# A one-core decoder layer: the convolution kernel's prologue in overlapping quarters, x loaded ahead of a zero fill, and the experts in groups of two and two batches instead of three and one

## The chip, the cores and the metric

One core of one Trainium2 chip runs the whole program in one launch. The metric is the device time of that launch in microseconds, the median of several runs. The kernel before takes 579.54 us (three runs, 575.65 to 581.82).

## The reference, cut to what matters

Four batches of 512 tokens of width 128 go through one decoder layer:

```python
y  = attention(x)            # 16 heads of 8, 4 KV heads, RMS-normed and rotated q/k, tanh soft cap 50, causal
x1 = layernorm(x + y)
# cross attention to 32 context rows -> FiLM scale and shift, on a state-space (S4D) long convolution
K  = 2 * Re(sum_n dC[d,n] * exp(dtA[d,n] * l))          # l = 0..511, the convolution kernel, from weights only
t  = causal_conv(modulate(layernorm(x1)), K) ...        # in the kernel: discrete Fourier transform, lags, back
h  = layernorm(t); ff = W2 gelu(W1 h); x2 = layernorm(...)
# mixture of experts: two shared experts on all tokens, 2 of 8 routed experts for each token
out = layernorm(x2 + shared(x2) + w_a * expert_a(x2) + w_b * expert_b(x2))
```

All of it is computed in both kernels. Nothing of the arithmetic's result is changed.

## The kernel before, in words

**Orders written out by hand.** Each of the four compute engines plays a list of named steps (`PE_ORDER`, `ACT_ORDER`, `DVE_ORDER`, `POOL_ORDER`, lines 75 to 183). A step is a small function with its own semaphore waits. An engine works strictly in the order of its list, so a step that waits holds all that stand behind it. `sc:b.p.n` is a fill of scores of batch b, head pair p; `tanh`, `exp` and `mask` are the softmax of that pair on ScalarE and GpSimd; `val:q` multiplies the probabilities of two pairs by the values; `xT`, `qkv`, `rms`, `rope`, `parts`, `copies`, `qT` prepare a batch; `rows`, `y`, `yT`, `proj`, `x1` finish its attention; `xs`, `attnT`, `film`, `mod`, `dft`, `lags`, `conv`, `shape` are cross attention, FiLM and the convolution; `h`, `hT`, `up`, `down`, `ffT`, `ffn`, `x2` the feed-forward; `gates`, `route`, `rank`, `place`, `scatter` the routing; `su`, `sd` the eight steps of the two shared experts; `bt`, `bu`, `bd` (transpose, up, down) with `bx`, `bg`, `by`, `store` are one block of 128 rows of a routed expert; `fetch`, `fin`, `settle`, `fo` gather and finish a batch. `val:15` is the last of the attention.

**The prologue of the convolution kernel.** K is built in four quarters q of 32 channels. GpSimd makes the angles (`angles`, L1019) and the exponents (`exps`, L1037), VectorE reduces the angles (`args`, L1303), ScalarE takes three sines and two exponentials (`powers`, L882), VectorE mixes (`powers`, L1318), GpSimd multiplies (`products`, L1029), TensorE multiplies 32 small matrices (`taps`, L632) and VectorE copies the result into `kij` (L1296). Angles and exponents share the tiles `pr` and `ue`, so that the exponents of a quarter wait for its `args`, and the angles of the next quarter for the `products`. After the fourth quarter SyncE writes `kij` to memory (256 KB) and reads it back in another layout. `tap` (L1340) builds the transform's tables and adds one row, `kernel:0/1` transform K, `spectra` and `spectra2` make the three spectra that `lags` needs. No batch can go past `dft` and `lags` without them.

**The loads.** SyncE issues all loads from one queue in the order of the code (L474 is the helper). x of batches 2 and 3 and the feed-forward weights `wt` stand behind a zero fill of 8.9 MB of `expert_rows`, the memory that the routed tokens are scattered to.

**The experts.** `GROUP = [0, 0, 0, 1]` (L53) runs the routed experts twice: for batches 0 to 2, and for batch 3. A group of n batches has `2 * n * SEQ / P + NE - 1` blocks (L57), the most that the routing can need: 31 and 15, 46 in all. SyncE loads a group's blocks (weights of 578 KB and rows of 64 KB for each, from six slots) once the group's block table is written and its last scatter has landed:

```python
            for g in range(GROUPS):
                sp.wait_ge(table_ready, g + 1)
                sp.wait_ge(scattered[g], 16 * 2 * NT * SIZE[g])
                for q in range(NB[g]):
                    load_block(BLOCK0[g] + q)
```

The block buffers share memory with tiles of the attention, so no block is loaded before `val:15` (L562). The gathers of a group's batches (`fetch`, L1115) wait for the stores of all its blocks.

## Time and profile before

| | |
|---|---|
| median of three runs | 579.54 us (575.65 to 581.82) |
| the profiled execution | 581.24 us, of which 579.5 us are the span that the profile shows |
| TensorE matmuls busy | 429.5 us (74%) |
| VectorE busy | 374.5 us (65%) |
| ScalarE busy | 328.0 us (57%) |
| GpSimd busy | 263.2 us (45%) |
| mean granted TensorE clock | 0.873 of full speed |
| memory traffic | 58.58 MB, mean 101 GB/s |

The profiled execution is one run, 1.7 us above the median of the three. Busy shares are averages over stages that differ: attention of batches 0 to 2 lies between 45 and 244 us of the span, that of batch 3 between 244 and 338 us, the routed experts from 422 us on.

### The profile page before, as it was taken

Reading aid. Unit: us, or ns where it says so; the run is one execution under the profiler, and the core shown is the slowest. Engines: PE = TensorE matmul, PEld = TensorE weight load, DVE = VectorE, ACT = ScalarE, POOL = GpSimd, SP = SyncE. Lnnn points to the kernel's source line nnn. Section 1 sums busy time; section 2 is a strip of 40 time slices with the busy share of each in tenths; the row PEclk is TensorE's granted clock in tenths of the full one; section 3 lists DMA queues with packets and bytes.
Section 4 is the critical chain, followed back from the end, with each engine's and each line's share of the span. In section 5 each row is a group of like instructions: output and inputs, shape, how many; then the busy total and the mean of one; then the engine's idle time right before and its main releaser. Section 6 shows DMA issues by size and latency. Waiting matters only on the chain.

```text
span 579.5 us, 9129 instructions
## 1 busy us (share of the span) xinstructions
PE 429.5 (74%) x2857; PEld 272.5 (47%) x2857; DVE 374.5 (65%) x1107; ACT 328.0 (57%) x563; POOL 263.2 (45%) x305
## 2 busy tenths in 40 slices
PE   3475646763776967789887988988888899888860
PEld 2252223440333624344333446455757887877750
DVE  1993885269872787887899599788711438124554
ACT  1046979895798798637784743614235356444420
POOL 2400876359694372244177645642610123107753
PEclk9977767786878687989877999999979999999985
DMA  3595000000000069400000100100178996888931
GB/s 99 170 421 220 2 1 3 0 1 0 1 2 1 1 156 195 89 2 0 2 1 0 37 2 1 36 2 0 38 235 255 303 307 196 282 284 260 315 88 41
DMA packets 43814, 58.58 MB, mean 101 GB/s; under 512 B 7531, under 2 KB 32870, under 8 KB 43750
## 3 DMA queue, kind: packets, MB, share of 16 engines
q1 hardware_dynamic: 35094, 50.78, 28.7%
q0 software_dynamic: 2048, 4.20, 2.4%
q10 hardware_dynamic: 6624, 3.02, 1.8%
q8 instruction: 24, 0.39, 0.3%
q14 instruction: 24, 0.20, 0.1%
HBM read 42.23 MB, written 20.46 MB: 108 GB/s over the span
## 4 chain that ended last, share of the span: by engine, by line
PE 28%; DVE 21%; SPq 12%; POOL 11%; ACT 10%; DMA 9%; issue 9%; POOLq 0%; DVEq 0%; ACTq 0%
SPq L474 9%; PE bank_o L699 6%; DMA x_blk<-expert_rows 5%; ACT probs L917 3%; PE ring_g L777 3%; PE ring_g L579 3%; DMA x<-in_x 3%; PE ring_g L782 2%; PE ring_s L685 2%; POOL probs L1071 2%; PE ring_g L749 2%; ACT probs L923 2%; PE ring_s L850 2%; SPq L555 2%; SPq L553 2%
## 5 line engine op out<-in xcount | busy, mean ns | idle before, releaser
L917 ACT ACTIVATE probs<-ring_s 128x512 f32<-128x512 f32 (+1 forms) x192 | 87.6, 542 | 38.7 <-PE ring_s L685 36.9
L1071 POOL TENSOR_SCALAR_AFFINE_SELECT probs<-probs 128x256 f32<-128x256 f32 (+1 forms) x96 | 54.6, 601 | 96.5 <-ACT probs L923 96.5
L966 ACT ACTIVATE g_ring<-ring_s,w_blk 128x128 f32<-128x128 f32 x184 | 52.0, 372 | 57.2 <-PE ring_s L850 51.3
L685 PE MATMUL ring_s<-qT,kT 64*128 64x256 bf16 (+3 forms) x256 | 55.3, 350 | 31.5 <-ACT probs L917 29.0
L923 ACT ACTIVATE probs<-probs 128x2560 f32<-128x2560 f32 x32 | 75.1, 2345 | 0.7
L699 PE MATMUL bank_o<-probs,vv 128*32 128x128 f32 (+3 forms) x512 | 55.1, 588 | 22.8 <-POOL probs L1071 22.6
L1017 POOL TENSOR_TENSOR rstd<-var_eps,neg_half 128x4 f32<-128x4 f32 x24 | 25.1, 1047 | 83.8 <-DVE var_eps L1379 75.9
L685 PEld LDWEIGHTS ring_s<-qT,kT 64*128 64x128 bf16 x256 | 16.2, 98 | 74.5 <-ACT probs L917 54.7
L850 PE MATMUL ring_s<-xT_blk,w_blk 128*128 128x128 f32 x368 | 48.3, 277 | 1.7 <-DVE xT_blk L1682 1.7
L858 PE MATMUL ring_g<-w_blk,g_ring 128*128 128x128 f32 x368 | 48.1, 277 | 0.6 <-ACT g_ring L966 0.6
L699 PEld LDWEIGHTS bank_o<-probs,vv 128*32 128x32 f32 x512 | 20.7, 138 | 57.1 <-issue 54.6
L1125 POOL DMA_INDIRECT y_pair<-expert_out,y_rows x32 | 30.9, 967 | 34.6 <-DMA expert_out<-y_blk 25.5
L850 PEld LDWEIGHTS ring_s<-xT_blk,w_blk 128*128 128x128 f32 x368 | 44.5, 192 | 4.1 <-issue 3.8
L1112 POOL DMA_INDIRECT expert_rows<-x,rows_i x32 | 31.6, 986 | 31.9 <-DVE rows_i L1661 23.3
L858 PEld LDWEIGHTS ring_g<-w_blk,g_ring 128*128 128x128 f32 x368 | 44.3, 192 | 1.9 <-issue 1.4
L959 ACT ACTIVATE g_ring<-ring_s,vcols 128x512 f32<-128x512 f32 x32 | 21.5, 690 | 38.2 <-PE ring_s L823 21.8
L1688 DVE TENSOR_TENSOR y_blk<-ring_g,w_blk 128x128 f32<-128x128 f32 x46 | 13.2, 289 | 34.4 <-PE ring_g L858 34.3
L1682 DVE COPY xT_blk<-ring_g 128x128 f32<-128x128 f32 x46 | 13.1, 287 | 33.1 <-PE ring_g L579 33.0
L832 PEld LDWEIGHTS bank_a<-w_sh,g_ring 128*128 128x128 f32 x256 | 30.8, 192 | 4.3 <-issue 4.3
L832 PE MATMUL bank_a<-w_sh,g_ring 128*128 128x128 f32 x256 | 31.7, 275 | 0.0
L823 PE MATMUL ring_s<-x2T,w_sh 128*128 128x512 f32 x64 | 31.3, 599 | 0.0
L579 PE MATMUL ring_g<-ident,x 128*128 128x128 f32 x48 | 8.9, 316 | 22.8 <-DMA x<-in_x 9.6
(342 smaller groups left out, 915.3 us busy)
## 6 DMA issues: line engine op xcount, KB each, us to landing
w_blk<-expert_pack SPq DMA_DIRECT2D x46, 578.0 KB, 5.1
expert_rows<-zero_rows SPq DMA_DIRECT2D x1, 6144.0 KB, 20.7
expert_pack<-in_L_ffn_W SPq DMA_DIRECT2D x16, 256.0 KB
x_blk<-expert_rows SPq DMA_DIRECT2D x46, 64.0 KB, 4.4
expert_out<-y_blk ACTq DMA_DIRECT2D x46, 64.0 KB, 4.7
expert_rows<-zero_rows SPq DMA_DIRECT2D x1, 2048.0 KB, 19.1
x<-in_x SPq DMA_DIRECT2D x4, 256.0 KB, 8.9
w_sh<-in_L_ffn_sW SPq DMA_DIRECT2D x4, 256.0 KB, 4.8
```

The source lines that it names most:

```text
L474: sp.dma_start(dst, src).then_inc(s, 16)
L685: last = mm(bank[:, c:c + w], kT[64 * r:64 * r + 64, p // 2, P * j:P * (j + 1)], qT[64 * r:64 * r + 64, p, P * j:SEQ], start=True, stop=True)
L699: last = mm(bank_o[32 * h:32 * h + 32, P * j:SEQ], vv[:, j, q, :], probs[:, (2 * quad + h // 2) % NPROB, c:c + SEQ - P * j], start=(j == 0 ...
L823: mm(bank[:, :], w_sh[:, e, P * n:P * (n + 1)], x2T[:, b, :], start=True, stop=True).then_inc(s_full, 1)
L832: last = mm(bank_a[:, P * j:P * (j + 1)], g[:, P * j:P * (j + 1)], w_sh[:, e, HID + P * n:HID + P * (n + 1)], start=(c == 0 and j == 0), s ...
L850: last = mm(bank[:, P * n:P * (n + 1)], w_blk[:, k % SLOTS, P * n:P * (n + 1)], xT_blk[:, k % RING, :], start=True, stop=True)
L858: last = mm(bank[:, 0:D], g[:, P * n:P * (n + 1)], w_blk[:, k % SLOTS, HID + HC + P * n:HID + HC + P * (n + 1)], start=(n == 0), stop=(n = ...
L917: f(probs[:, pair % NPROB, BASE[n]:BASE[n] + WIDTH[n]], s_bank("sc", b, p, n)[:, 0:WIDTH[n]], ACT.Tanh, scale=1.0 / (CAP * float(np.sqrt(n ...
L923: f(probs[:, pair % NPROB, :], probs[:, pair % NPROB, :], ACT.Exp, scale=CAP).then_inc(exp_done, 1)
L966: last = f(g_ring[:, u % RING, P * n:P * (n + 1)], s_bank("bu", k)[:, P * n:P * (n + 1)], ACT.Gelu, bias=w_blk[:, k % SLOTS, HID + n:HID + ...
L1071: last = g.affine_select(out=v, in_=v, compare_op=ALU.is_ge, fill=0.0, base=0, pattern=[[0, v.shape[1]], [1, P]], channel_multiplier=-1)
L1112: g.indirect_dma_start(out=rows_dram, out_offset=bass.IndirectOffsetOnAxis(ap=rows_i[:, k, b * NT + j:b * NT + j + 1], axis=0), in_=x2[:, ...
```

## The change

There are three edits, and all four lists are written anew. The numbers of instructions of each step stay the same but for the spectra.

```diff
-GROUP = [0, 0, 0, 1]
+GROUP = [0, 0, 1, 1]
...
-            kld = pv[:, 0:NT * D // JM, :].rearrange("p a c -> p (a c)").rearrange("p (j d) -> p j d", j=NT)
+            pe_arg = tb("pe_arg", [P, JM, JM])
+            ue_arg = tb("ue_arg", [P, JM, IM])
+            kld_rows = tb("kld_rows", [P, NT, D])
+            kld = kld_rows[:, :, :]
...
-            kij = tb("kij", [IM, JM, D])
+            kij = tb("kij", [IM, 2, JM, JM])
...
-            load_x(1)
+            for b in range(1, B):
+                load_x(b)
+            load(wt[:, 0:HID], t["L0_xattn_W1"], ld_wt)
+            load(wt[:, HID:2 * HID].rearrange("p (c d) -> p c d", c=HC),
+                 t["L0_xattn_W2"].rearrange("(c p) d -> p c d", p=P), ld_wt)
...
-            for b in range(2, B):
-                load_x(b)
-            load(wt[:, 0:HID], t["L0_xattn_W1"], ld_wt)
-            load(wt[:, HID:2 * HID].rearrange("p (c d) -> p c d", c=HC),
-                 t["L0_xattn_W2"].rearrange("(c p) d -> p c d", p=P), ld_wt)
-            sp.wait_ge(*g_freed("taps", D // JM - 1, 1))
-            load(kernel_dram.rearrange("(i j) d -> i (j d)", i=IM), kij.rearrange("i j d -> i (j d)"), kij_sent)
-            sp.wait_ge(kij_sent, 16)
+            for q in range(D // JM):
+                sp.wait_ge(*g_freed("taps", q, 1))
+                load(kernel_dram.rearrange("(i j) d -> i j d", i=IM)[:, :, JM * q:JM * (q + 1)], kij[:, q % 2, :, :], kij_sent[q % 2])
+            for n in range(2):
+                sp.wait_ge(kij_sent[n], 16 * (D // JM // 2))
...
-            def powers(q):
+            def sines(q):
                 if q:
                     act.wait_ge(g_full, g_done(f"taps:{q - 1}.1"))
-                act.wait_ge(pro_arg, 3 + 2 * q)
-                f(pv[:, :, :], pt[:, :, :], ACT.Sin, scale=-SIN_SCALE, bias=offs[:, 2:3]).then_inc(pro_fun, 1)
                 act.wait_ge(pro_arg, 4 + 2 * q)
+                f(pv[:, :, :], pt[:, :, :], ACT.Sin, scale=-SIN_SCALE, bias=offs[:, 2:3])
                 f(uf[:, :, :], uf[:, :, :], ACT.Sin, scale=-SIN_SCALE, bias=offs[:, 2:3])
-                f(ug[:, :, :], ug[:, :, :], ACT.Sin, scale=-SIN_SCALE, bias=offs[:, 3:4]).then_inc(pro_fun, 1)
+                f(ug[:, :, :], ug[:, :, :], ACT.Sin, scale=-SIN_SCALE, bias=offs[:, 3:4]).then_inc(sines_ready, 1)
+
+            def decays(q):
                 act.wait_ge(exponents_ready, q + 1)
-                f(pr[:, :, :], pr[:, :, :], ACT.Exp)
-                f(ue[:, :, :], ue[:, :, :], ACT.Exp).then_inc(pro_fun, 1)
+                f(pe_arg[:, :, :], pe_arg[:, :, :], ACT.Exp)
+                f(ue_arg[:, :, :], ue_arg[:, :, :], ACT.Exp).then_inc(decays_ready, 1)
```

On GpSimd `exps(q)` writes the new tiles and waits for the `products` of the quarter before (for `packed` in the first), `angles(q)` waits for the first part of `args` of that quarter, `products(q)` for `sines` and `decays`. On VectorE `args(q, 0)` waits in addition for the sines of the quarter before, and `evac` of quarters 2 and 3 for the store of the quarter two before. `tap` is split: the tables (`ctabs`, nine instructions) stand early in the list, behind `bias`, and only the added row stays. The two spectra steps (ten instructions) become one of seven:

```diff
-                op(ts(re[:, 1:NT, :], ks[:, 0:NT - 1, :], lag_sign[:, 1:2], None, ALU.mult))
-                one(ts(im[:, 1:NT, :], kc[:, 0:NT - 1, :], lag_sign[:, 0:1], None, ALU.mult))
-                op(tt(re[:, 1:NT, :], re[:, 1:NT, :], kc[:, 1:NT, :], ALU.add))
-                one(tt(im[:, 1:NT, :], im[:, 1:NT, :], ks[:, 1:NT, :], ALU.add))
+                op(stt(out=re[:, 1:NT, :], in0=n[:, 0:NT - 1, :], scalar=lag_sign[:, 1:2], in1=c[:, 1:NT, :], op0=ALU.mult, op1=ALU.add))
+                stt(out=im[:, 1:NT, :], in0=c[:, 0:NT - 1, :], scalar=lag_sign[:, 0:1], in1=n[:, 1:NT, :], op0=ALU.mult, op1=ALU.add).then_inc(g_freed("kernel", 1)[0], 1)
```

**The lists.** The group change makes 23 and 23 blocks, `table:0` and `yplaces:0` stand behind batch 1's routing and `fetch:2.*` behind block 45. In TensorE's list `taps:0` to `taps:3` stand at pairs 0.5, 0.7, 1.1/1.2 and 1.4 (before: 0.5/0.6, 1.1/1.2, 1.6, 2.1), `kernel:0` at 1.6 (before 2.4), `film:0` at 1.7/2.0 (before 2.6), `dft:0` at 2.2 (before 2.7), `hT:0` just ahead of `sc:3.0.0` (before just behind `sc:3.0.5`). Ahead of `val:15` the list before has these steps, and the new one has them behind it: `gates:0 rank:0 hT:1 up:1.0-3 down:1.0-3 ffT:1 dft:2.0-2 conv:2.0 su:0.0-2`; VectorE's list has moved the steps that go with them (`route:0` to `select:0`, `lags:2.*`, `ffT:1`, `ffn:1`). Ahead of `rank:3` it no longer has `su:2.5-7 su:3.0-2 sd:2.3-7 bu:15-19 bd:14-19 bt:18-23`. An excerpt of the new list, around the first blocks:

```
su:1.5 sd:1.2 su:1.6 ffT:2 sd:1.3 su:1.7 sd:1.4 conv:3.0 conv:3.1 sd:1.5 conv:3.2 bt:0 bt:1 sd:1.6 sd:1.7 bu:0 bu:1
bt:2 bt:3 bt:4 bu:2 bu:3 bd:0 bd:1 bd:2 bu:4 bd:3 bt:5 x2T:2 bu:5 bd:4 bt:6 gates:2 hT:3 bu:6 bd:5 up:3.0 up:3.1
...
bd:40 bt:42 su:3.0 bd:41 bt:43 bu:42 sd:3.0 bt:44 bu:43 bu:44 bt:45 bd:42 bu:45 bd:43 bd:44 bd:45 su:3.1 su:3.2 su:3.3
sd:3.1 sd:3.2 sd:3.3 su:3.4 su:3.5 su:3.6 sd:3.4 sd:3.5 sd:3.6 su:3.7 sd:3.7
```

## Rows read from the trace of the kernel before

**Rows 1.** Busy time by stage: stretch, length, busy and count by engine, PEclk, DMA share, GB/s
```profile
45.20:244.10 198.90, 132.79 (x1050) 66.61 (x1050) 134.59 (x282) 162.73 (x224) 110.70 (x123) 0.77 0.20 45
244.10:337.90 93.80, 79.89 (x394) 36.34 (x395) 75.24 (x214) 59.37 (x83) 49.20 (x57) 0.87 0.02 6
337.90:421.70 83.80, 72.19 (x410) 47.96 (x410) 70.40 (x234) 29.74 (x42) 44.84 (x40) 1.00 0.04 14
421.70:559.50 137.80, 121.40 (x914) 106.59 (x914) 55.96 (x232) 63.85 (x201) 40.14 (x41) 0.98 0.82 262
559.50:579.50 20.00, 0.03 (x1) 0.00 (x0) 7.64 (x26) 0.00 (x0) 8.85 (x10) 0.55 0.20 54
```

**Rows 2.** Timelines of TensorE and ScalarE: start, length, instruction, in brackets idle before
```profile
51.25 1.09 PE L579 MATMUL ring_g<-ident,x 128*128 128x128 f32 x4 [6.38 <-DMA x<-in_x]
...
52.91 1.15 ACT L917 ACTIVATE probs<-ring_s 128x512 f32<-128x512 f32 x3 [5.73 <-PE ring_s L685]
```

**Rows 3.** The chain of waits around 36 us: start, length, what
```profile
36.52 14.60 DMA x<-in_x
```

**Rows 4.** Timeline of SyncE's queue, the zero fill
```profile
21.48 14.99 SPq L474 DMA_DIRECT2D expert_rows<-zero_rows  x4
```

**Rows 5.** Timeline of VectorE, the tables inside `tap`, first and last of six
```profile
211.45 1.75 DVE L1330 TENSOR_TENSOR conv_tab<-waves 128x128 f32<-128x128 f32 x1
...
214.69 0.50 DVE L1337 TENSOR_SCALAR conv_tab<-conv_tab 128x128 f32<-128x128 f32 x3
```

**Rows 6.** Waits: ScalarE from 45 to 244 us; then GpSimd, whole span: total, times, longest
```profile
ACT probs L917 <- PE ring_s L685: 27.8, 12, 8.8
...
POOL pv L1032 <- ACT ue L892: 12.7, 3, 7.1
...
POOL uf L1034 <- DVE uf L1322: 5.4, 2, 4.1
```

**Rows 7.** One source line, the first multiply of `rope`: min/median/max in ns, first and last start
```profile
L1054 POOL TENSOR_TENSOR qkv<-qkv,rms_out x16: 457/550/1735, 20.2 to 207.8; 128x160 f32<-128x160 f32 x16
```

**Rows 8.** Groups of TensorE's instructions, 312 to 342 us: busy, mean ns of one, idle before
```profile
L777 PE MATMUL ring_g<-hT,wt 128*128 128x512 f32 x8 | 4.2, 629 | 0.0
L782 PE MATMUL ring_g<-g_raw,wt 128*128 128x512 f32 x8 | 3.6, 592 | 0.0
L754 PE MATMUL ring_g<-xn,conv_tab 128*128 128x512 f32 x6 | 3.2, 610 | 0.0
L823 PE MATMUL ring_s<-x2T,w_sh 128*128 128x512 f32 x6 | 3.0, 610 | 0.0
```

**Rows 9.** Busy time of VectorE alone in one stretch, the step `lags:2.0`
```profile
330.10:333.50 3.40, 3.17 (x7) 1.00 0.12 39
```

**Rows 10.** The chain of waits, two `su` steps and two `bd` steps
```profile
553.16 1.72 PE ring_s L823 x4
...
554.88 1.80 PE ring_g L858 x16
```

**Rows 11.** Timeline of GpSimd: last of eight scatters of batch 2, of batch 3
```profile
418.32 0.96 POOL L1112 DMA_INDIRECT expert_rows<-x,rows_i  x1 [0.30 <-issue]
...
495.36 0.96 POOL L1112 DMA_INDIRECT expert_rows<-x,rows_i  x1 [0.31 <-issue]
```

**Rows 12.** One tile, the 46 block transposes (`bt`)
```profile
L579 PE MATMUL ring_g<-ident,x_blk x46: 272/299/421, 427.6 to 550.1; 128*128 128x128 f32 x46
```

**Rows 13.** Timeline of SyncE's queue: first and fifth of five loads of block rows
```profile
504.28 0.35 SPq L474 DMA_DIRECT2D x_blk<-expert_rows  x1
...
513.83 0.34 SPq L474 DMA_DIRECT2D x_blk<-expert_rows  x1
```

**Rows 14.** Timeline of the end: last stores, first and last of eight gathers of batch 3
```profile
556.66 0.81 ACTq L974 DMA_DIRECT2D expert_out<-y_blk  x2
...
559.78 1.00 POOL L1125 DMA_INDIRECT y_pair<-expert_out,y_rows  x1 [0.19 <-issue]
...
568.69 0.95 POOL L1125 DMA_INDIRECT y_pair<-expert_out,y_rows  x1 [0.31 <-issue]
```

More of the change, by code:

```diff
@@ L96 @@
-ffT:0 dft:1.1 sc:3.2.3 sc:3.2.4 val:12 sc:3.2.5 sc:3.3.0 sc:3.3.1 dft:1.2 sc:3.3.2 conv:1.0 conv:1.1 sc:3.3.3 sc:3.3.4
-sc:3.3.5 sc:3.4.0 sc:3.4.1 sc:3.4.2 conv:1.2 sc:3.4.3 attnT:2 rows:12 sc:3.4.4 sc:3.4.5 sc:3.5.0 sc:3.5.1 sc:3.5.2
-film:2.0 film:2.1 film:2.2 sc:3.5.3 sc:3.5.4 sc:3.5.5 x2T:0 film:2.3 sc:3.6.0 sc:3.6.1 sc:3.6.2 gates:0 val:13 hT:1
-sc:3.6.3 sc:3.6.4 sc:3.6.5 rank:0 up:1.0 up:1.1 sc:3.7.0 sc:3.7.1 up:1.2 val:14 up:1.3 rows:13 down:1.0 down:1.1
-down:1.2 down:1.3 rows:14 dft:2.0 ffT:1 sc:3.7.2 sc:3.7.3 sc:3.7.4 dft:2.1 sc:3.7.5 su:0.0 su:0.1 dft:2.2 su:0.2
@@ L101 @@
-conv:2.0 val:15 conv:2.1 sd:0.0 su:0.3 su:0.4 conv:2.2 rows:15 sd:0.1 su:0.5 sd:0.2 yT:3 su:0.6 x2T:1 proj:3 sd:0.3
-gates:1 su:0.7 sd:0.4 sd:0.5 sd:0.6 x1T:3 sd:0.7 rank:1 hT:2 xs:3 su:1.0 su:1.1 su:1.2 up:2.0 up:2.1 up:2.2 su:1.3
-up:2.3 attnT:3 down:2.0 down:2.1 down:2.2 down:2.3 film:3.0 film:3.1 ffT:2 film:3.2 film:3.3 sd:1.0 sd:1.1 sd:1.2
-sd:1.3 dft:3.0 dft:3.1 dft:3.2 su:1.4 su:1.5 conv:3.0 su:1.6 sd:1.4 su:1.7 conv:3.1 sd:1.5 sd:1.6 sd:1.7 x2T:2
-conv:3.2 gates:2 su:2.0 su:2.1 su:2.2 rank:2 su:2.3 sd:2.0 su:2.4 sd:2.1 sd:2.2 sd:2.3 sd:2.4 su:2.5 su:2.6 su:2.7
@@ new lines @@
+sc:3.6.1 sc:3.6.2 conv:1.0 conv:1.1 conv:1.2 sc:3.6.3 sc:3.6.4 sc:3.6.5 val:14 sc:3.7.0 sc:3.7.1 sc:3.7.2 rows:13
+attnT:2 sc:3.7.3 sc:3.7.4 rows:14 sc:3.7.5 film:2.0 film:2.1 film:2.2 film:2.3 x2T:0 val:15 gates:0 hT:1 rows:15
+su:0.0 up:1.0 yT:3 up:1.1 su:0.1 up:1.2 proj:3 rank:0 sd:0.0 up:1.3 sd:0.1 down:1.0 down:1.1 down:1.2 down:1.3 x1T:3
+dft:2.0 dft:2.1 dft:2.2 su:0.2 su:0.3 su:0.4 conv:2.0 su:0.5 sd:0.2 ffT:1 conv:2.1 sd:0.3 sd:0.4 conv:2.2 sd:0.5 xs:3
+su:0.6 su:0.7 sd:0.6 sd:0.7 attnT:3 film:3.0 film:3.1 film:3.2 film:3.3 x2T:1 gates:1 su:1.0 su:1.1 su:1.2 hT:2 su:1.3
@@ L151 @@
+sg:3.3 sg:3.4 sg:3.5 sg:3.6 sg:3.7
 """
 DVE_ORDER = """
-rms:0 vectors rroot:0 fold1 vv:0 bias fold2 parts:0 fold3 steps copies:0 fold4:0 fold4:1 fold4:2 states states2
-states3 pack rms:1 fold4:3 rroot:1 args:0.0 args:0.1 args:0.2 oT:0 y:0 parts:1 copies:1 oT:1 powers:0 y:1 evac:0.0
-evac:0.1 args:1.0 args:1.1 args:1.2 oT:2 y:2 vv:1 oT:3 powers:1 y:3 rms:2 yT:0 rroot:2 evac:1.0 args:2.0 evac:1.1
-args:2.1 proj:0 args:2.2 parts:2 oT:4 x1:0 copies:2 xnorm:0 y:4 oT:5 xn:0 powers:2 scores:0 y:5 soften:0 evac:2.0
@@ L157 @@
-args:3.0 evac:2.1 args:3.1 args:3.2 oT:6 y:6 oT:7 vv:2 powers:3 y:7 yT:1 rms:3 proj:1 evac:3.0 evac:3.1 rroot:3 x1:1
-xnorm:1 oT:8 tap y:8 parts:3 spectra copies:3 spectra2 oT:9 film:0.0 film:0.1 film:0.2 film:0.3 mod:0 y:9 oT:10
-lags:0.0 lags:0.1 lags:0.2 xn:1 scores:1 shape:0 oT:11 vv:3 soften:1 y:10 y:11 hnorm:0 yT:2 h:0 film:1.0 film:1.1
-proj:2 film:1.2 hT:0 film:1.3 mod:1 x1:2 xnorm:2 scores:2 lags:1.0 lags:1.1 ffT:0 lags:1.2 ffn:0 soften:2 oT:12
-shape:1 xn:2 y:12 x2n:0 hnorm:1 x2:0 film:2.0 film:2.1 film:2.2 h:1 film:2.3 mod:2 gates:0 route:0 hT:1 weights:0
@@ L172 @@
-fin:3.0 fin:3.1 fin:3.2 fin:3.3 fo:3
+rms:0 vectors rroot:0 fold1 bias ctabs fold2 parts:0 fold3 steps copies:0 vv:0 fold4:0 fold4:1 states fold4:2 states2
+states3 pack rms:1 fold4:3 rroot:1 args:0.0 args:0.1 args:0.2 parts:1 powers:0 args:1.0 copies:1 args:1.1 oT:0
+evac:0.0 args:1.2 y:0 evac:0.1 oT:1 args:2.0 powers:1 y:1 args:2.1 oT:2 evac:1.0 y:2 args:2.2 evac:1.1 args:3.0 vv:1
+powers:2 oT:3 args:3.1 y:3 rms:2 yT:0 rroot:2 args:3.2 proj:0 evac:2.0 evac:2.1 oT:4 powers:3 parts:2 x1:0 copies:2
@@ new lines @@
+y:15 route:0 yT:3 weights:0 proj:3 place:0 select:0 x1:3 xnorm:3 lags:2.0 lags:2.1 lags:2.2 ffT:1 shape:2 xn:3
+scores:3 ffn:1 hnorm:2 soften:3 settle:0 x2n:1 film:3.0 film:3.1 x2:1 film:3.2 h:2 film:3.3 mod:3 gates:1 route:1 hT:2
+weights:1 place:1 select:1 table:0 yplaces:0 lags:3.0 lags:3.1 lags:3.2 ffT:2 shape:3 bx:0 bx:1 ffn:2 settle:1 hnorm:3
+bx:2 bx:3 bx:4 x2n:2 by:0 by:1 x2:2 by:2 h:3 bx:5 by:3 by:4 bx:6 gates:2 hT:3 route:2 by:5 weights:2 place:2 select:2
+bx:7 by:6 ffT:3 bx:8 bx:9 by:7 ffn:3 bx:10 bx:11 bx:12 by:8 x2n:3 by:9 bx:13 x2:3 by:10 by:11 by:12 by:13 gates:3
```

210 lines of the change are left out of this document (109 added, 101 removed).

## The prediction

> **What bounds the kernel now.** I read the busy time by stage first. No single engine bounds the whole. While batches 0 to 2 are in attention, ScalarE is busy 162.7 of 198.9 us and TensorE 132.8, at a granted clock of 0.77; while batch 3 is, TensorE is busy 79.9 of 93.8, VectorE 75.2 and ScalarE only 59.4; behind it TensorE leads again, 72.2 of 83.8 and 121.4 of 137.8; and the last 20.0 us have no matmul work at all [rows 1]. So a microsecond of work moved out of the third stage shortens it, and comes back later as work on the same engine. That makes the question one of idle time: which of TensorE's gaps does the change close, and which does it open?
>
> The timelines say what the first gap is. TensorE sits idle for 6.4 us and ScalarE for 5.7, until x of batch 2 is there [rows 2]; the load is on the chain of waits with 14.6 us [rows 3], because it is issued behind a zero fill that alone takes 15.0 us to issue [rows 4]. The waits show the second kind: ScalarE's tanh waits 27.8 us for scores between 45 and 244 us, up to 8.8 us at a time, and GpSimd, with the masks queued behind it, waits 12.7 and 5.4 us for the two inputs of `products` [rows 6]. The last views are of the end. The 46 blocks are transposed from 427.6 to 550.1 us, 2.72 us each [rows 12], 9.3 us behind the last scatter issue of batch 2 [rows 11, 12]. After the last store come eight gathers and the finish of batch 3 [rows 14].
>
> **x ahead of the fill.** The four loads (x of batches 2 and 3, two of `wt`) move ahead of the tables and the fill. The 6.4 us go; what is late next is `pack` on TensorE, which waits for VectorE's state steps. Into those comes the work of the tables: 211.45 to 215.19, 3.7 us [rows 5], now ahead of the first scores, where VectorE has little room. Net gain 6.4 - 3.7 = 2.7 us. Bounds: 6.4 gained if the tables fit into gaps, 3.7 lost if the stall only changes its name; if the tables' own loads, now behind 1 MB more, land late, it is the lower end. The fill itself ends later by four issues; the first scatter, which waits for it, comes only when batch 0 is routed, so three batches of attention hide it. Without that cover it would cost four issues, under 2 us if each takes a tenth of the fill's 15.0 or less.
>
> **Overlapping quarters.** Instruction counts stay: five activations a quarter on ScalarE, `args`, `powers` and `evac` on VectorE, `angles`, `exps`, `products` on GpSimd. What changes is who holds whom. Exponents no longer wait for `args`, so the exponentials are long done when `products` comes up, and the masks behind it are freed. The most that this can give is the two waits, 12.7 + 5.4 = 18.1 us [rows 6]; the least is nothing, or a loss, since the same work now lies in a shorter stretch. Most of such a wait would be replaced by the next one, for ScalarE is busy 82% of that stage. I take 4 us, nearer the lower end for that reason. The spectra are three instructions shorter and `kernel` stands six pairs of scores earlier, but `dft:0` moved ahead only fills the gaps of a stage bound elsewhere; I cost both at nothing on the path. The four small stores of `kij` and their waits stand on SyncE ahead of the packing of the expert weights, which nobody needs until the shared experts; the last one and the read back take the place of the old pair. Nothing, hidden by the 12 score fills and more that stand between `taps:3` and `kernel`.
>
> How GpSimd bears overlap can be bounded: the same multiply takes 0.46 us at best and 1.74 at worst [rows 7], 1.28 us more. The Trainium skill (SBUF — State Buffer, two separate sides) says that VectorE with two inputs in SBUF and GpSimd share one port pair under an exclusive lock, and that the loser blocks for the whole instruction. By that rule overlap is paid with such waits; it speaks against this part, and the spread of the row agrees with it without proving it.
>
> **The work behind `val:15`.** Ahead of `val:15` the list loses four `up`, four `down`, three `dft`, three `su`, one `conv` and a few short ones. By the groups the first four are 4.2 + 3.6 + 3.2 + 3.0 = 14.0 us, the `conv` is as long as a `dft`, 1.1 [rows 8]: 15.1 us. VectorE loses as much or more, three `lags` of 3.2 [rows 9] and the steps that route batch 0. At the stage's density (79.9 / 93.8 = 0.85) attention ends 15.1 / 0.85 = 17.8 us earlier. ScalarE, at 59.4 us, is the floor of the stage, and leaves room for it. The work returns later at (72.2 + 121.4) / 221.6 = 0.87, so 17.3 us [rows 1]. By itself this part is worth 0.5 us; it matters in that experts can start in the middle of the batches' work.
>
> **Two and two.** The blocks stay 46. The second group now has 23, and two batches of gathers follow it. I go along that group from the last scatter of batch 3, as if it came no earlier: issue at 495.4 [rows 11], 9.3 us to the first transpose as in batch 2's case, 504.6. Then 22 spacings: at best 2.39 us, SyncE's rate ((513.83 - 504.28) / 4) [rows 13], at worst 2.72 [rows 12]. I take 2.55, the middle, since 2.72 holds a pause for batch 3 and 2.39 holds none: 56.1 us, bounds 52.6 and 59.8. Last transpose to last store 556.7 - 550.1 = 6.6, from there to the end 22.8, and the eight gathers of batch 2 that now stand in the same tail, 568.69 + 0.95 - 559.78 = 9.9 us [rows 14]. Sum 504.6 + 56.1 + 6.6 + 22.8 + 9.9 = 600.0 us. So this part costs 20.5 us unless batch 3 is routed earlier.
>
> How much earlier? The list has taken six `su`, five `sd`, five `bu`, six `bd` and six `bt` from ahead of `rank:3`: 6 x 0.86 + 16 x 0.90 + 6 x 0.30 = 21.4 us [rows 10, 12], at the stage's density of 121.4 / 137.8 = 0.88 it is 24.3. With 2.7 and 4 from the start that is 31.0 us, and the end is 600.0 - 31.0 = 569.0.
>
> **A second sum as a check**, by TensorE's whole work: 2.7 and 4 earlier, 17.8 gained and 17.3 given back. Behind `bd:45` there now stand seven `su` and seven `sd`, 12.3 us, and they lie beside the gathers. The tail from the last store, 22.8 + 9.9 = 32.7, is thus 20 us behind TensorE's last work, as now. That gives 579.5 - 7.2 = 572. The first sum goes along what ends last, so I stay near it: 570.5 us of span, 9 less than before. The profiled execution has 581.24 us around its span of 579.5, and stands 1.7 above the median of the three; the difference taken from the median gives 579.5 - 9 = 570.5, and I round to 570.
>
> **Rivals.** (1) *The prologue was the hidden bound.* If all 18.1 us of GpSimd's waits [rows 6] leave ScalarE's path instead of 4, the end is 14 lower: 556. For it: ScalarE waits 27.8 us in that stage, up to 8.8 at once. Against it: it is 82% busy, and `rope` still holds the masks at each change of batch. (2) *The overlap is eaten on GpSimd.* Its prologue has 24 instructions, and at 1.28 us each [rows 7] at most 31 us are lost. A third of it, 10 us, in place of the 4 won, would give 570 + 14 = 584 if all were on the path; with half on it, 577 to 580. That is the port rule of the Trainium skill (SBUF — State Buffer) at work. No change in the time. (3) *The second group becomes the bound, and it is slower.* Its place is SyncE's wait for the scatter of batch 3; its price is the 20.5 us above. It decides when that scatter comes less than 20.5 us earlier than now. If batch 3's own chain (projection, cross attention, convolution, feed-forward, each a trip through four engines) is what times it, and TensorE merely idles where the blocks were, only the 6.7 us of the start count: 600.0 - 6.7 = 593. For it: TensorE has little else to do there than wait for VectorE, 70.4 of 83.8 busy. Against it: in the list before, `ffT:3` stands behind twelve block transposes, so batch 3 had slack there. (4) *The x load does nothing*, since the tables take its place: 2.7 less, within the forecast's width.
>
> **Chances.** Forecast 0.48 (563 to 577), rival 1 0.18 (556), rival 2 0.20 (577 to 584), rival 3 0.14 (593). A measurement of this kernel tells about 1% from no change, so faster is below 573.7 and slower above 585.3. Of the forecast I count 0.38 below, and 0.03 of rival 2; with rival 1 that is 0.59. Same: 0.26. Slower: rival 3 and a little, 0.15. The range leaves out most of rival 3 and the lower tail of rival 1: 552 to 585.
>
> **What would show it.** ScalarE goes on with its tanh 2 to 3 us earlier than 52.9, with no wait for x, and GpSimd's waits at `products` are gone; if they are and batch 3's first scores do not come earlier still, the 4 us were wrong. `val:15` starts at 313 us, not 338. The first block's transpose comes before 405, and there is a pause in TensorE's blocks between the 23rd and the 24th. The last scatter starts near 464, the last transpose near 531, the last store near 538, then 33 us to the end without blocks. The prediction is wrong if the scatter of batch 3 comes later than 475, or if the spacing of the last 22 blocks is outside 2.4 to 2.7.

## The result and the profile after

The changed kernel takes 553.78 us (median of four runs, 553.21 to 555.19). The kernel before, with a fourth run beside it, takes 578.0 (575.65 to 581.82). The ratio is 0.958, 95% interval 0.952 to 0.964: 4.2% faster. The forecast was 570, so 1.6% faster. The sign was right, and the time lies inside the stated range of 552 to 585, near its lower end; the size forecast was less than half of what came.

The profiled execution has a span of 551.5 us, 28.0 below the 579.5 before. First the page, then the busy time by stage, with the stages cut as in [rows 1].

```profile
span 551.5 us, 9139 instructions
PE 413.4 (75%) x2857; PEld 266.1 (48%) x2857; DVE 373.3 (68%) x1104; ACT 324.7 (59%) x561; POOL 258.1 (47%) x305
...
DVE 42%; PE 20%; issue 10%; POOL 8%; DMA 6%; ACT 6%; SPq 6%; DVEq 0%; POOLq 0%; ACTq 0%
```

```profile
44.20:232.90 188.70, 132.59 (x1120) 68.50 (x1118) 146.04 (x322) 167.04 (x229) 114.17 (x129) 0.81 0.21 51
232.90:294.70 61.80, 53.09 (x314) 22.96 (x312) 47.92 (x127) 50.70 (x72) 29.71 (x42) 0.92 0.00 1
294.70:373.10 78.40, 70.20 (x334) 41.63 (x333) 68.28 (x222) 27.05 (x38) 36.24 (x32) 0.93 0.10 31
373.10:532.10 159.00, 140.85 (x1047) 123.09 (x1045) 71.97 (x299) 72.53 (x213) 59.48 (x59) 0.98 0.71 222
532.10:551.50 19.40, 0.00 (x0) 0.00 (x0) 9.07 (x31) 0.00 (x0) 8.84 (x9) 0.57 0.20 54
```

Compare them with [rows 1]. Attention of batches 0 to 2 ends 11.2 us earlier (232.9 for 244.1). Batch 3's attention is 32.0 us shorter (61.8 for 93.8), with 26.8 us less TensorE work in it at the same density, 0.86. ScalarE, busy 50.7 of 61.8 us, is now nearly as full as TensorE there. All that follows is longer: 221.6 us before up to the last matmul, 237.4 now. So the gain lies wholly ahead of `val:15`, and some of it is given back behind.

The waits of ScalarE and GpSimd between 44 and 233 us, to be held against [rows 6]:

```profile
ACT probs L922 <- PE ring_s L689: 13.1, 11, 3.1
...
POOL uf L1041 <- DVE uf L1334: 5.9, 2, 4.0
POOL pr L1031 <- DVE uf L1328: 5.1, 2, 4.5
...
POOL pv L1039 <- ACT ug L892: 3.3, 1, 3.3
```

ScalarE's wait for scores is less than half of what it was, and the wait at the first product of a quarter fell from 12.7 to 3.3. The other wait at `products` is still there (5.9 us, 5.4 before), and the angles (L1031) wait 5.1 us for VectorE where they waited 0.6. The end, to be held against [rows 11, 12, 14]: the last scatter issue of batch 3; the tile of the 46 block transposes; the last three stores together (their last is issued at about 518.0); the first gather of batch 2.

```profile
441.73 0.96 POOL L1121 DMA_INDIRECT expert_rows<-x,rows_i  x1 [0.30 <-issue]
...
516.22 2.33 ACTq L979 DMA_DIRECT2D expert_out<-y_blk  x3
...
520.76 1.00 POOL L1134 DMA_INDIRECT y_pair<-expert_out,y_rows  x1 [29.53 <-issue]
```

```profile
L583 PE MATMUL ring_g<-ident,x_blk x46: 272/273/329, 373.1 to 512.8; 128*128 128x128 f32 x46
```

The last scatter is 53.6 us earlier (forecast 31.0), the last transpose 37.3, the end 28.0. From the last scatter to the end 25.6 us of the gain are thus lost, where the forecast lost 20.5.

### The profile page after: what moved, and what is told of

The parts are those of the page before. It is cut to its first block, busy times and chain, and to the rows that moved or that the text cites. A ratio compares the mean times of both kernels' runs of the same rounds, so it can differ in the third digit from the quotient of the medians.

```text
span 551.5 us, 9139 instructions
## 1 busy us (share of the span) xinstructions
PE 413.4 (75%) x2857; PEld 266.1 (48%) x2857; DVE 373.3 (68%) x1104; ACT 324.7 (59%) x561; POOL 258.1 (47%) x305
## 4 chain that ended last, share of the span: by engine, by line
DVE 42%; PE 20%; issue 10%; POOL 8%; DMA 6%; ACT 6%; SPq 6%; DVEq 0%; POOLq 0%; ACTq 0%
POOL y_pair L1134 4%; SPq L477 3%; DMA x_blk<-expert_rows 3%; PE ring_g L781 3%; PE ring_s L854 2%; PE ring_g L862 2%; DVE stats L1383 2%; PE ring_g L753 2%; PE ring_g L786 2%; DMA y_pair<-expert_out,y_rows 2%; DVE hn L1394 2%; PE ring_g L583 2%; PE bank_o L703 2%; DVE g_raw L1544 2%; ACT probs L928 2%
## 5 line engine op out<-in xcount | busy, mean ns | idle before, releaser
L971 ACT ACTIVATE g_ring<-ring_s,w_blk 128x128 f32<-128x128 f32 x184 | 52.1, 370 | 65.2 <-PE ring_s L854 44.6
L1080 POOL TENSOR_SCALAR_AFFINE_SELECT probs<-probs 128x256 f32<-128x256 f32 (+1 forms) x96 | 50.8, 559 | 58.5 <-ACT probs L928 58.5
L689 PE MATMUL ring_s<-qT,kT 64*128 64x512 bf16 (+3 forms) x256 | 52.2, 340 | 28.8 <-ACT probs L922 24.3
L854 PE MATMUL ring_s<-xT_blk,w_blk 128*128 128x128 f32 x368 | 50.3, 283 | 3.3 <-DVE xT_blk L1691 3.2
L703 PE MATMUL bank_o<-probs,vv 128*32 128x128 f32 (+3 forms) x512 | 45.8, 506 | 8.0 <-POOL probs L1080 6.3
L854 PEld LDWEIGHTS ring_s<-xT_blk,w_blk 128*128 128x128 f32 x368 | 46.3, 198 | 6.6 <-issue 6.3
L703 PEld LDWEIGHTS bank_o<-probs,vv 128*32 128x32 f32 x512 | 16.7, 122 | 37.4 <-issue 32.6
L1711 DVE SCALAR_TENSOR_TENSOR x<-y_pair,w_sel,x 128x128 f32<-128x128 f32 x32 | 11.2, 350 | 22.2 <-DMA y_pair<-expert_out,y_rows 21.5
## 6 DMA issues: line engine op xcount, KB each, us to landing
w_blk<-expert_pack SPq DMA_DIRECT2D x46, 578.0 KB, 4.6
```

Of the source, the lines that this page charges most:

```text
L689: last = mm(bank[:, c:c + w], kT[64 * r:64 * r + 64, p // 2, P * j:P * (j + 1)], qT[64 * r:64 * r + 64, p, P * j:SEQ], start=True, stop=True)
L703: last = mm(bank_o[32 * h:32 * h + 32, P * j:SEQ], vv[:, j, q, :], probs[:, (2 * quad + h // 2) % NPROB, c:c + SEQ - P * j], start=(j == 0 ...
L854: last = mm(bank[:, P * n:P * (n + 1)], w_blk[:, k % SLOTS, P * n:P * (n + 1)], xT_blk[:, k % RING, :], start=True, stop=True)
L971: last = f(g_ring[:, u % RING, P * n:P * (n + 1)], s_bank("bu", k)[:, P * n:P * (n + 1)], ACT.Gelu, bias=w_blk[:, k % SLOTS, HID + n:HID + ...
L1080: last = g.affine_select(out=v, in_=v, compare_op=ALU.is_ge, fill=0.0, base=0, pattern=[[0, v.shape[1]], [1, P]], channel_multiplier=-1)
```

## The experiments

Twelve kernels ran in three groups of four, each group on one chip beside the kernel before. On those chips the kernel before took 603, 600 and 601 us in place of 578, so I compare within a group, and by ratio across. In the table "attention" is the end of batch 3's last exponential, "batches 0 to 2" that of batch 2's, and "rest" is the span less "attention". All times are of the profiled execution, the ratio with its interval is of the timed runs.

| kernel | batches 0 to 2 | attention | rest | span | ratio to before |
|---|---|---|---|---|---|
| before (first chip) | 244.1 | 336.3 | 243.2 | 579.5 | 1 |
| after (first chip) | 232.9 | 290.7 | 260.8 | 551.5 | 0.958 (0.952 to 0.964) |
| new_head_old_rest | 234.4 | 291.8 | 290.0 | 581.8 | 0.974 (0.965 to 0.984) |
| old_head_new_rest | 240.4 | 333.0 | 278.4 | 611.4 | 1.017 (1.009 to 1.025) |
| put_off_only | 240.1 | 320.5 | 294.6 | 615.1 | 1.030 (1.020 to 1.039) |
| late_x | 235.0 | 292.3 | 284.7 | 577.0 | 0.962 (0.954 to 0.969) |
| after_again | 234.9 | 292.3 | 279.2 | 571.5 | 0.960 (0.951 to 0.969) |
| batch3_as_before | 234.0 | 326.8 | 274.6 | 601.4 | 1.007 (1.003 to 1.011) |
| batch3_as_after | 237.1 | 316.9 | 280.0 | 596.9 | 1.003 (0.999 to 1.008) |
| quarters_in_turn | 246.3 | 303.7 | 279.2 | 582.9 | 0.974 (0.969 to 0.978) |
| after_third | 234.6 | 291.9 | 278.2 | 570.1 | 0.951 (0.948 to 0.955) |
| tables_in_gap | 232.3 | 289.7 | 277.5 | 567.2 | 0.951 (0.946 to 0.957) |
| tables_and_sines | 232.5 | 289.9 | 283.0 | 572.9 | 0.952 (0.949 to 0.956) |
| tables_sines_copies | 233.3 | 290.7 | 277.6 | 568.3 | 0.954 (0.951 to 0.958) |

Two columns tell the story. "Attention" comes out the same on all four chips for the new head (290.7, 291.8, 292.3, 291.9). The old head is less even: its lists up to the last exponential of batch 2 are the same in four kernels, and these end batch 2 at 244.1, 240.4, 240.1 and 237.1. So what the new head wins in batches 0 to 2 is 11.2 us on the first chip, 5 to 6 on the second and 2.2 on the third (237.1 for 234.9); why it spreads stays open. From there to the end of `val:15` the old head takes 96.1 and 97.0 us, the new one 64.2 and then 62.2 or 62.3 in each run, so these lengths can be compared. "Rest" is 275 to 285 for every kernel with the new lists behind attention, whatever stands ahead; on the first chip it was 18 us less (more of that at the end).

### Head or rest

new_head_old_rest: the changed loads, prologue and lists up to the last step of attention, then the old order and three and one.

```
-GROUP = [0, 0, 1, 1]
+GROUP = [0, 0, 0, 1]
 behind val:15, exp:31, oT:15, mask:31: the steps in the order of the kernel before
```

> The changed kernel's loads, prologue and lists up to the last product of the attention (val:15), then the old kernel's order of all that is left, with the experts in groups of three and one again. Theory A (the gain is made ahead of val:15, by the prologue, the x load and the lists of the attention, and the groups are about even): val:15 starts near 295 us as in the changed kernel, and the rest takes the old 241.6 us plus 17 to 20 for the steps that were put off, so 553 to 558 us in all, ratio to before 0.955 to 0.97. Theory B (the two groups of two batches are what turns the earlier attention into an earlier end): val:15 near 295, but the end at 565 to 572.

old_head_new_rest: the mirror. Five steps of batch 2's convolution and its neighbours had to stay directly behind `val:15`.

```
-GROUP = [0, 0, 0, 1]
+GROUP = [0, 0, 1, 1]
 behind val:15, exp:31, oT:15, mask:31: the steps in the order of the changed kernel
```

> The old kernel's loads, prologue and lists up to val:15, then the changed kernel's order of the rest with groups of two and two. Theory A: val:15 near 338 us, the rest 256.8 us as in the changed kernel less the 17 to 20 us of steps that are already done, so 575 to 580 us, no change. Theory B: 560 to 568 us, since the blocks start some 20 us earlier in the batches' work.

The head alone gives 2.6%, the rest alone costs 1.7%, both together give 3.8% on this chip (late_x, below) and 4.0 to 4.9% on the others. The sum of the two parts would be 0.9%, so they need each other. The reason is in the column "rest": behind the new head the old order takes 290.0 us and the new one 284.7 on the same chip (late_x), while behind the old head the new order takes 278.4 and the old one about 265 to 268. The last is an estimate: 603 us, less 1.8 around the span, less the 333 to 336 of the old head's attention. Of the expectations, the ratio of new_head_old_rest is between theory A (up to 0.97) and theory B (0.98 and more), and old_head_new_rest, slower than before, meets neither. No kernel changes the groups and leaves the lists, or the other way round, so what the two groups alone are worth stays open.

### The deferral alone

put_off_only: the kernel before, with the 19 steps of TensorE (and what belongs to them elsewhere) moved behind `val:15`.

```
-... x2T:0 film:2.3 ... gates:0 val:13 hT:1 ... rank:0 up:1.0 up:1.1 ... su:0.2 conv:2.0 val:15
+... x2T:0 film:2.3 ... val:13 ... val:14 ... val:15 gates:0 hT:1 rank:0 up:1.0 ... su:0.2 conv:2.0
```

> The old kernel, with one thing of the change alone: the 19 TensorE steps that the change moved behind val:15 (gates:0, rank:0, hT:1, up:1, down:1, ffT:1, dft:2, conv:2.0, su:0.0 to 0.2) and the VectorE, ScalarE and GpSimd steps that go with them are moved there; old prologue, old loads, groups of three and one. If moving them is what shortens batch 3's attention, val:15 starts 18 to 27 us earlier than 338 and the end changes by under 3 us (they come back). If the earlier attention needs the earlier convolution kernel, val:15 moves by under 10 us and the end is later, by up to 10.

Attention ends 12 to 16 us earlier, and yet the kernel is 3% slower, since its rest is 294.6 us, for the 265 to 268 just estimated. Put off under the old order, the steps delay the routing of batches 0 to 2, and three batches' blocks with it: the last scatter of batch 2 is issued at 428.3 us, 418.3 in the first profile of the kernel before. They come back at 26 to 30 us. Both expectations fail: `val:15` starts 15.8 us earlier, between the "under 10" and the "18 to 27", and the end is later by more than either allowed.

### Which part of the head

late_x: the changed kernel with x of batches 2 and 3 and the two of `wt` behind the zero fill again.

```
-            for b in range(1, B):
-                load_x(b)
-            load(wt[:, 0:HID], t["L0_xattn_W1"], ld_wt)
...
+            load_x(1)
...
+            for b in range(2, B):
+                load_x(b)
+            load(wt[:, 0:HID], t["L0_xattn_W1"], ld_wt)
...
```

> The changed kernel with x of batches 2 and 3 and the feed-forward weights loaded behind the zero fill again, nothing else. If the x load is worth what the stall showed, 6.4 us less the 3.7 of the tables, TensorE waits for x again until about 51 us and the whole is 2 to 5 us longer (556 to 559). If the stall is hidden by the state steps that pack waits for, it is within 1 us of the changed kernel.

Attention ends at 292.3, to 0.1 us where after_again has it on another chip, and the ratios are 0.962 and 0.960. The load ahead of the fill is worth nothing that I can see, as the second branch of the expectation had it: `xT:2` stands behind the six pairs of scores of mask 0 in the new list and starts at 52.1 us in either kernel.

after_again: the changed kernel as it is, for the other three of its group.

> The changed kernel once more, as it stands, so that the other three of this group have it on their own chip. Both theories: attention ends (last exponential of batch 3) at 290 us, as in its first profile, and 0.955 to 0.970 of the kernel before. What it tells apart is the chip: the earlier group had a kernel before of 603 us in place of 578, and the spacing of the last 22 expert blocks was 3.1 us there in place of 2.75. If the stage of the experts is what differs between chips, the first 290 us are the same here again.

batch3_as_before: the changed kernel, with the order of the kernel before from the last exponential of batch 2 to that of batch 3. The same steps as in the old head are kept directly behind `val:15`.

```
 ... sc:2.7.5 | xs:1 val:11 qT:3.3 rows:10 ... hT:0 ... gates:0 val:13 hT:1 ... rank:0 up:1.0 ... conv:2.0 val:15 | conv:2.1 ...
   new order  | order of before                                                                        | new order
```

> The changed kernel, with the steps between the last exponential of batch 2 and the last of batch 3 in the order that they had before: the 19 steps of TensorE (experts' gates, the feed-forward of batch 1, the spectra of batch 2, the first shared expert) stand inside batch 3's attention again, with what belongs to them on the other engines. Batches 0 to 2 and all that follows stay as changed. Theory P (my terms: the deferral is worth what it takes out of batch 3): batch 3's attention, 57.8 us now and 92.2 before, comes to 57.8 + 17.8 = 76 us or more, so attention ends near 309, and the time is little changed, since the work is gone later: 0.96 to 0.975 of before. Theory Q (the work pulled ahead of batch 2's end is what counts): 63 to 70 us, near 300. A rival, that batch 3 was slow only because of the steps' order: over 85 us, ending at 318 or later, 0.985 or more.

batch3_as_after: its mirror. The loads, prologue and order of before up to the last exponential of batch 2, and the changed order with two groups of two from there.

```
 ... sc:2.7.5 | conv:0.0 conv:0.1 conv:0.2 rows:10 xs:1 ... hT:0 qT:3.5 sc:3.0.0 ... x2T:0 val:15 gates:0 hT:1 ...
  order before| order of after
```

> The mirror of it: the kernel before with its own loads, prologue and lists up to the last exponential of batch 2, and from there the changed lists and two groups of two. The convolution of batch 0 is thus not pulled ahead; it stands in batch 3's attention, with nothing deferred work there. Theory P: 92.2 - 17.8 = 74 us of batch 3's attention behind an end of batch 2 at 240 to 244 us: 315 us, and 0.98 to 0.99 of before. Theory Q: over 78 us, as in the kernel with the deferral alone (80.4), and 0.99 to 1.00. If the order of the steps alone is what helps: under 65 us, 305, and 0.965 to 0.975.

Busy time from batch 2's last exponential to the end of `val:15`, in this order: the kernel before, batch3_as_before, batch3_as_after, put_off_only, after_again. Columns as in [rows 1].

```profile
244.10:340.20 96.10, 82.19 (x423) 37.44 (x423) 77.25 (x221) 60.93 (x85) 50.34 (x57) 0.88 0.02 6
```

```profile
234.00:330.70 96.70, 80.78 (x411) 35.93 (x411) 67.49 (x192) 60.04 (x83) 42.37 (x52) 0.85 0.02 6
```

```profile
237.10:323.30 86.20, 66.40 (x369) 30.22 (x369) 58.14 (x159) 51.63 (x72) 38.50 (x48) 0.78 0.00 1
```

```profile
240.10:326.00 85.90, 67.30 (x369) 29.86 (x369) 60.78 (x159) 51.69 (x73) 39.77 (x48) 0.82 0.00 1
```

```profile
234.90:297.10 62.20, 53.92 (x345) 23.42 (x343) 49.15 (x130) 51.30 (x73) 31.37 (x43) 0.95 0.00 1
```

Read the length and the first pair. Under the old order the deferral takes 15 us of TensorE's work out, as I had counted, and shortens the stretch by 10 us (96 to 86). The earlier first three batches, with the old order and without the deferral, win nothing in this stretch (96.7). All together it is 62. So the gain of 34 us is a joint one.

It is joint of three things, though, and not of two: batch 0's convolution ahead of the stretch, the deferral, and the order of the steps inside the stretch. The last is new in batch3_as_after and after_again and old in the other three. With the new order and the deferral in both, the earlier convolution is worth 24 us (86.2 to 62.2); without it, the new order is worth nothing over the old one (86.2 for 85.9). No kernel has the early convolution and the deferral under the old order, so how much of the 34 us belongs to the deferral and how much to the order is not shown.

Of the expectations, P, my own counting, fails in both kernels. Up to the last exponential batch 3's attention takes 92.8 us in batch3_as_before, which is the rival's "over 85" (the order of the steps), with its end at 326.8 and its ratio of 1.007 as that rival had them. It takes 79.8 in batch3_as_after, Q's "over 78", and there the order alone does not help. Either kernel loses all of the 4%.

What happens at the change of batch is in TensorE's timelines, of batch3_as_after, after_again and batch3_as_before (start, length, instruction, in brackets the idle time before).

```profile
234.81 1.10 PE L760 MATMUL ring_g<-g_raw,conv_tab 128*128 128x512 f32 x2 [1.17 <-DVE g_raw L1537]
238.19 2.08 PE L760 MATMUL ring_g<-g_raw,conv_tab 128*128 128x512 f32 x2 [2.29 <-DVE g_raw L1537]
241.36 2.07 PE L760 MATMUL ring_g<-g_raw,conv_tab 128*128 128x512 f32 x2 [1.09 <-DVE g_raw L1537]
...
255.77 1.03 PE L674 MATMUL ring_g<-identb,k_parts 128*128 128x128 bf16 x8 [5.91 <-DVE y_att L1467]
258.05 1.09 PE L579 MATMUL ring_g<-ident,hn 128*128 128x128 f32 x4 [1.25 <-POOL hn L1079]
...
259.92 1.03 PE L685 MATMUL ring_s<-qT,kT 64*128 64x512 bf16 x4
```

```profile
234.76 0.62 PE L678 MATMUL ring_g<-identb,k_parts 128*128 128x128 bf16 x8 [1.41 <-DVE y_att L1476]
235.36 0.66 PE L583 MATMUL ring_g<-ident,hn 128*128 128x128 f32 x4
...
236.88 0.59 PE L689 MATMUL ring_s<-qT,kT 64*128 64x512 bf16 x4 [0.38 <-ACT kT L915]
```

```profile
237.89 4.49 PE L702 MATMUL bank_o<-probs,vv 128*32 128x512 f32 x32 [6.06 <-POOL probs L1079]
...
245.56 0.39 PE L688 MATMUL ring_s<-qT,kT 64*128 64x512 bf16 x2 [0.38 <-ACT kT L914]
```

In the first, each of the three inverse transforms waits for VectorE's `lags`, then the keys of batch 3 wait for VectorE behind them, and the first scores come at 259.9, 22.8 us into batch 3. In the second the transforms are over by 220 us, and the first scores come at 236.9, 2.0 us in. These 20.8 us are most of the 24.0 between the two kernels. The third has the early convolution too, and still its first scores come at 245.6, 11.6 us in: in the order of before `val:11` stands ahead of the scores, and TensorE waits 6.1 us there for the last masks of batch 2. The new list has `val:11` behind five of the six score fills of the first pair. So the early convolution opens this place only together with the new order.

The lengths of the two parts, ahead of the first scores of batch 3 and from there to the end of `val:15`, say the same (us, from the same traces):

| kernel | convolution of batch 0 | order in the stretch | deferral | ahead | behind |
|---|---|---|---|---|---|
| before | late | old | no | 12.3 | 83.8 |
| put_off_only | late | old | yes | 12.2 | 73.6 |
| batch3_as_before | early | old | no | 11.6 | 85.2 |
| batch3_as_after | late | new | yes | 22.8 | 63.4 |
| after_again | early | new | yes | 2.0 | 60.3 |

With the old order the place ahead of the scores costs 12 us in each of the three kernels. The cell that was not run, early convolution and deferral under the old order, would be 11.6 + 73.6 = 85 us if the parts add; that is an estimate, and by it the order is the larger part of the gain. One limit: batch3_as_after runs an order that was made for an early filter, and pays more at this place than the kernel before.

quarters_in_turn: the changed kernel with one wait put back. The exponents of quarters 1 to 3 wait for the arguments again.

```
                 else:
                     pool.wait_ge(pro_sb, 3 + q)
+                    pool.wait_ge(pro_arg, 4 + 2 * q)
```

> The changed kernel with the overlap of the quarters taken back by one wait: GpSimd's exponents of quarters 1 to 3 wait for VectorE's arguments of the same quarter again, as before, so that the masks queued behind them wait too. Theory P (quarters are worth 4 us): attention ends 3 to 5 us later, at 294, the time 0.5 to 1% above the changed kernel's. Rival (the quarters were never on the path, or all on it): under 1 us of difference in the end of attention, or 10 us and more with waits of GpSimd at the exponents over 10 us in total.

The waits, from the first exponential to the last of batch 2: two lines of quarters_in_turn, one of after_again.

```profile
POOL pe_arg L1051 <- DVE uf L1329: 19.7, 3, 7.8
...
ACT pe_arg L896 <- POOL ue_arg L1051: 13.9, 3, 5.5
```

```profile
ACT pe_arg L896 <- POOL ue_arg L1050: 1.1, 1, 1.1
```

GpSimd waits 19.7 us for VectorE, ScalarE 13.9 us for GpSimd, batch 2 ends 11.4 us later and so does all that follows (span 582.9 for 571.5); the medians are 583.7 and 575.9, or 573.2 without the longest of the four runs of after_again. Undoing the overlap thus costs 8 to 11 us, where I had 4, and the second form of the rival in the expectation came (10 us and more, with over 10 us of waits at the exponents). Batch 3's stretch is untouched (62.2 us in both). One limit: the list is one that was made for the overlap, and without it batch 2 ends at 246.3, later than in any kernel with the old head (237.1 to 244.1). So this is what the new list would lose, and not what the old one would win.

### A version that goes further

after_third is the changed kernel once more. The three others move the tables and two neighbours of quarter 1.

> The changed kernel once more, to have it on the same chip as the three variants of it. Expected as before: attention ends at 290 to 293 us, ratio 0.955 to 0.965.

tables_in_gap:

```
-rms:0 vectors rroot:0 fold1 bias ctabs fold2 ... evac:1.1 args:3.0
+rms:0 vectors rroot:0 fold1 bias fold2 ... evac:1.1 ctabs args:3.0
```

> The changed kernel with VectorE's convolution tables moved from ahead of the state steps to behind the evacuation of quarter 1, where VectorE idles for 7 us. My step of the x load took 3.7 us off for these tables. Theory (they hold pack back): TensorE's pack and the first exponential come 2.5 to 3.5 us earlier, attention ends as much earlier, the time is 0.4 to 0.6% below the changed kernel's. Rival (the first scores wait for something else, such as x's transposes or the states): pack earlier, but the first exponential under 1 us earlier, and no change in the time.

tables_and_sines, in addition on ScalarE:

```
-decays:1 sines:1 tanh:0.5.4 tanh:0.5.5 qT:1.0 exp:5
+decays:1 tanh:0.5.4 tanh:0.5.5 qT:1.0 exp:5 sines:1
```

> As the one before, and ScalarE's sines of quarter 1 stand behind the exponential of mask 5 instead of ahead of its last two tanh. In the changed kernel that exponential takes 17.9 us from the one before it, with 4.2 us of ScalarE's idle time ended by VectorE's arguments of the quarter. Theory (a wait at the head of ScalarE's queue counts in full): attention ends 4 to 6 us earlier than with the tables alone. Rival (the next step waits in its place, since VectorE's mixing of the same quarter comes later too): under 1.5 us, with a longer wait of GpSimd at the products of quarter 1.

tables_sines_copies, in addition on VectorE:

```
-args:1.0 copies:1 args:1.1 oT:0 evac:0.0 args:1.2
+args:1.0 args:1.1 oT:0 evac:0.0 args:1.2 copies:1
```

> As the one before, and VectorE's copies of batch 1's parts (6.4 us) stand behind the arguments of quarter 1 instead of between their second and third part. Theory (VectorE's order is what makes the quarter late): the sines come 5 us earlier, attention ends 1 to 3 us earlier than without it. Rival: the queries of batch 1, which need the copies, come later by as much and take it back: no change or 1 to 3 us later.

TensorE's transposes of `pack`, and ScalarE's first exponential, in after_third and in tables_in_gap:

```profile
49.35 0.66 PE L583 MATMUL ring_g<-ident,packs 128*128 128x128 f32 x4
...
53.24 2.41 ACT L928 ACTIVATE probs<-probs 128x2560 f32<-128x2560 f32 x1
```

```profile
46.41 0.76 PE L583 MATMUL ring_g<-ident,packs 128*128 128x128 f32 x4
...
50.32 2.41 ACT L928 ACTIVATE probs<-probs 128x2560 f32<-128x2560 f32 x1
```

Both come 2.9 us earlier, and attention ends 2.2 us earlier: my 3.7 us for the tables at that place were right to within one. The time is 569.9 us against 571.7 (ratios 0.951 both, intervals overlapping), so a gain of 0.3% is likely by the trace and not shown by the measured time. The other two give nothing, as the rivals of their expectations had it: attention ends 0.2 and 1.0 us later than with the tables alone. Moving ScalarE's sines took away its wait and moved it to GpSimd: between 60 and 125 us the wait at the first product is 4.8 us with the sines moved, 2.5 without.

```profile
POOL pv L1039 <- ACT ug L892: 4.8, 2, 2.5
```

```profile
POOL pv L1039 <- ACT ug L892: 2.5, 1, 2.5
```

No version beats the changed kernel by more than its measurement can tell.

## Why the prediction was off, step by step

**The load of x (forecast 2.7 us).** Wrong in its reason, small in size. The load's place is worth nothing (late_x); the wait on x went because the list no longer asks for batch 2's x before the first six pairs of scores. The tables cost 2.9 us there and not 3.7, and the first tanh starts 4.9 us later (50.1 for 45.2). The first exponential ends 1.0 us earlier in all (55.7 for 56.7).

**Overlapping quarters (forecast 4 us; failed as a term).** Undoing the overlap costs 11.4 us of attention. I argued that a wait would be replaced by the next one because ScalarE was 82% busy. A part of that did come (the angles wait 5.1 us for 0.6), but most did not: ScalarE's exponentials wait 13.9 us for GpSimd without the overlap and 1.1 with it. ScalarE's wait for scores, which fell from 27.8 to 13.1, is mostly not the overlap's (17.0 without it, 14.6 with it, both under the new list). What the first three batches won in all, this part and the loads, is less sure: 11.2 us on the first chip and 2.2 on the third, where I had 6.7. They hold more work now, batch 0's convolution.

**"`dft:0` moved ahead only fills the gaps of a stage bound elsewhere; I cost both at nothing on the path" (this is the step that failed most).** The filter is ready 47 us earlier (the first `kernel` matmul at 169 for 216), so batch 0's convolution ends before batch 3 begins. Under the new order that is worth 24 us of batch 3's attention, 20.8 of them ahead of the first scores; under the old order, without the deferral, it is worth nothing. I had looked for the gap that it fills and not at the place that it leaves: there it stood as a chain TensorE to VectorE and back at the change of batch, ahead of the first scores. And the new order inside the stretch, `val:11` behind the first scores among it, has no term in the forecast at all, though the early convolution is worth nothing without it or the deferral.

**The work behind `val:15` (forecast 17.8 us out, 17.3 back; failed on both sides).** Out: 15 us of TensorE's work, as counted, shorten the stretch by 10 us alone (put_off_only, 85.9 for 96.1) and by 34 us with the earlier convolution and the new order (62.2 for 96.7). Back: little. With the new order the rest takes 274.6 us when the steps are already done (batch3_as_before) and 279.2 when they come back (after_again), 4.6 us in place of 17.3; on another chip it is 278.4 and 284.7 (old_head_new_rest, late_x), 6.3 us. Under the old order it takes 26 to 30 us more (put_off_only). I priced the return by TensorE's density. My reading, which no run isolates, is that the order in which batches 2 and 3 pass through the engines sets that stage, and that the steps go into its pauses or into its path according to where they stand.

**Two and two (forecast: 20.5 us dearer, less what batch 3 gains).** Right in sum. From the end of `val:15` (340.2 before, so 315.7 by my 24.5 us, and 569.0 as the end) I forecast 253 us; it took 254.4 (551.5 - 297.1), 239.3 before. From the last scatter to the end I forecast 104.6 and it took 109.8: 22 spacings of 2.75 us (452.3 to 512.8), and the 0.20 us over my 2.55 in each are 4.4 of the 5.2. That spacing is just outside the 2.4 to 2.7 that I had named as a sign of being wrong. That the sum is right to 1 us is luck. From the end of `val:15` to that of `rank:3` it is 132.9 us for 144.3, 11.4 less, where my terms gave 17.3 back and 24.3 off, 7.0 less. With a return of 4.6 the shared experts and blocks taken from ahead of `rank:3` gave 16.0 and not 24.3. So the return was 12.7 too dear, this gain 8.3 too large and the last group 5.2 too cheap.

**The sum.** Forecast up to `val:15`: 24.5 us. Measured: 43.1 (297.1 for 340.2). The missing 18.6 us are nearly the whole difference between the forecast span of 570.5 and 551.5. Of them 4.5 lie in batches 0 to 2 (11.2 for 6.7, and fewer on the other chips), and 14.1 in batch 3's attention (31.9 for 17.8), where I had a term for the deferral alone.

**The rivals.** Rival 1 (the prologue as hidden bound) had the better number, 556, but that is luck: its 14 us were to come out of the prologue, and 14.1 of the missing 18.6 lie in batch 3's attention, which it says nothing of. Of its reason, undoing the overlap shows up to 11.4 us of its 18.1. Rival 2 (GpSimd loses to the overlap) falls. The first multiplies of `rope` are faster than in [rows 7], and GpSimd is busy 258.1 us for 263.2:

```profile
L1063 POOL TENSOR_TENSOR qkv<-qkv,rms_out x16: 461/464/1440, 20.2 to 202.1; 128x160 f32<-128x160 f32 x16
```

The rule of the Trainium skill on which it leaned (SBUF — State Buffer, two separate sides) may well hold; the spread of 461 to 1440 ns agrees with it without proving it. By these figures the overlap did not add such meetings. Rival 3 (second group as the bound, slower) did not come: batch 3's scatter came 53.6 us earlier, far past its deciding point of 20.5. But old_head_new_rest, at 1.017, looks like that rival: its batch 3 is scattered at 483.9 us, 11.5 earlier than in the first profile of the kernel before, and without the shorter attention the new rest, groups and lists together, loses. Rival 4 (the load does nothing) was right.
